# Routing by a sorted top-8 and a 32-wide weight row, with denominators moved inside SBUF and three stores moved, in a linear-attention and expert layer

## The reference, cut to what matters

```
x = x + layernorm(attention(layernorm(x)))
x = x + layernorm(ffn(layernorm(x)))

attention: q, k, v of 16 heads of 32; rope on q and k
  phi(t)  = exp(features(t) - |t|^2 / 2)          # 128 features for each head
  numer   = phi(q) @ sum_tokens(phi(k) v)
  denom   = max(phi(q) . sum_tokens(phi(k)), 1e-6)
  out     = (numer / denom) @ w_out.T

ffn: scores = sigmoid(X @ gate_w.T)               # 32 experts
  idx  = top_k(scores + bias, 4);  w = scores[idx] / sum(scores[idx])
  pos  = how many earlier (token, choice) pairs took the same expert
  kept = pos < 512                                # capacity of an expert
  out  = sum over kept choices of w * W2(silu(W1 x) * W3 x)  +  a shared expert
```

## Time and profile before

| | us |
|---|---|
| median of three runs (2088.13 to 2090.12) | 2089.63 |
| the profiled execution's own time | 2089.07 |
| its span, first to last instruction | 2087.3 |
| projection, about | 0 to 585 |
| sums over the keys, about | 585 to 830 |
| attention and routing, up to the last send | 830 to 1414 |
| experts, up to the landing of the last add | 1414 to 1892 |
| combination | 1892 to 2087 |

### The profile page before, as it was taken

The page is one execution under the profiler, slowest core; times in us unless marked ns, Lnnn a source line. Parts: engine busy times, 40 slices in busy tenths (PEclk is TensorE's granted clock), DMA queues, the critical chain, the costliest instruction groups (busy, mean ns, idle before and its releaser), DMA issues.

```text
span 2087.3 us, 33721 instructions
## 1 busy us (share of the span) xinstructions
PE 1819.7 (87%) x12976; PEld 889.0 (43%) x12976; DVE 1207.8 (58%) x2230; ACT 1124.8 (54%) x1371; POOL 758.3 (36%) x718
## 2 busy tenths in 40 slices
PE   8999999999969998897888887455999989987795
PEld 5444444444448785132333333222444444443331
DVE  6776767676620000376888898861444344445786
ACT  5565555555436665586778775513444444432443
POOL 0000000000000000015877787874777777761110
PEclk9999999999979999999999999777999999999997
DMA  7445444446368885768877775342999999987983
GB/s 249 165 137 184 143 177 143 178 139 212 107 173 211 211 212 133 171 206 180 244 220 222 230 221 186 137 171 79 203 206 234 242 241 241 202 147 243 344 292 129
DMA packets 188848, 405.15 MB, mean 194 GB/s; under 512 B 33812, under 2 KB 72084, under 8 KB 172064
## 3 DMA queue, kind: packets, MB, share of 16 engines
q1 hardware_dynamic: 83184, 222.41, 35.6%
q10 hardware_dynamic: 68640, 124.26, 17.3%
q0 software_dynamic: 36864, 56.32, 14.4%
HBM read 237.06 MB, written 177.08 MB: 198 GB/s over the span
## 4 chain that ended last, share of the span: by engine, by line
PE 13%; DMA 12%; DVE 12%; issue 10%; POOL 9%; ACT 4%; SPq 1%; POOLq 0%; DVEq 0%; ACTq 0%
POOL slot_dram L1260 4%; DMA acc_dram<-s_y,s_slot 3%; PE s_gates L1485 3%; PE s_ups L1485 3%; PE s_ys L1500 2%; DMA s_spread<-share_dram 2%; DMA s_rows<-rows_dram,s_slot 2%; POOL acc_dram L1426 2%; DMA den_dram<-s_den 2%; PE s_turned L1462 1%; DVE s_stats L1651 1%; ACT s_xT L1531 1%; DVE s_x L1670 1%; POOL s_rows L1412 1%; PE s_y L898 1%
## 5 line engine op out<-in xcount | busy, mean ns | idle before, releaser
L258 PE MATMUL s_proj<-s_xT,keep_wqkv 128*128 128x512 f16 x1536 | 341.8, 379 | 0.0
L1260 POOL DMA_INDIRECT slot_dram<-keep_filled,keep_slots x256 | 292.1, 1141 | 105.2 <-issue 74.4
L1426 POOL DMA_INDIRECT acc_dram<-s_y,s_slot x128 | 205.1, 1603 | 93.0 <-issue 35.6
L258 PEld LDWEIGHTS s_proj<-s_xT,keep_wqkv 128*128 128x128 f16 x1536 | 147.8, 98 | 183.2 <-issue 12.6
L898 PE MATMUL s_y<-keep_wo,s_at_hl 128*128 128x512 f16 x768 | 188.6, 398 | 36.9 <-ACT s_z L988 36.9
L1540 ACT ACTIVATE s_gate<-s_gates 128x512 f32<-128x512 f32 x96 | 57.1, 597 | 263.8 <-PE s_ups L1485 218.4
L1610 DVE SCALAR_TENSOR_TENSOR s_h<-s_gate,s_ups 128x512 f32<-128x512 f32 x96 | 65.9, 686 | 216.1 <-ACT s_gate L1540 216.1
L339 POOL TENSOR_SCALAR s_rstd<-s_mv 128x4 f32<-128x4 f32 x16 | 16.0, 998 | 458.9 <-DVE s_mv L354 458.9
L676 ACT ACTIVATE s_phi<-s_logits 128x1024 f32<-128x1024 f32 x128 | 131.1, 1024 | 83.9 <-PE s_logits L697 83.9
L237 PE MATMUL s_proj<-keep_wqkv,s_xT 128*128 128x512 f16 x768 | 173.8, 383 | 1.2 <-ACT s_xT L500 1.2
L967 ACT ACTIVATE s_phi<-s_logits 128x1024 f32<-128x1024 f32 x128 | 131.4, 1027 | 63.5 <-PE s_logits L867 62.6
(11 more groups left out here) (165 smaller groups left out, 3202.8 us busy)
## 6 DMA issues: line engine op xcount, KB each, us to landing
s_x<-x_in SPq DMA_DIRECT2D x32, 1024.0 KB, 11.9
qk_dram<-s_hl ACTq DMA_DIRECT2D x32, 1024.0 KB, 6.0
keep_ahead<-qk_dram SPq DMA_DIRECT2D x48, 512.0 KB
acc_dram<-s_zero SPq DMA_DIRECT2D x17, 1024.0 KB, 13.9
v_dram<-s_v ACTq DMA_DIRECT2D x16, 1056.0 KB, 6.9
s_v<-v_dram SPq DMA_DIRECT2D x16, 1056.0 KB, 11.2
s_spread<-share_dram SPq DMA_DIRECT2D x64, 256.0 KB
x_dram<-s_x ACTq DMA_DIRECT2D x16, 1024.0 KB, 5.6
```

Source lines behind the costliest of these rows:

```text
L258: mm = nc.tensor.matmul(out[:, 512 * b:512 * b + 512], left, right, start=(c == 0 and i == 0), stop=(c == EC - 1 and i == 2))
L1260: nc.gpsimd.indirect_dma_start(out=io["slot"], out_offset=bass.IndirectOffsetOnAxis(ap=slots[n % 2][:, a * K + j:a * K + j + 1], axis=0), ...
L1426: nc.gpsimd.indirect_dma_start(out=io["acc"], out_offset=bass.IndirectOffsetOnAxis(ap=slot[e % RING][:, a, 0:1], axis=0), in_=y[e % 2][:, ...
```

## The change

What is computed stays the same; the data that the last two stages hand over has another shape.

- **Top four by replacement.** `choose` takes the eight largest values of a row (as before), then replaces the four largest of them in a copy with a marker (`match_replace`, whose list of eight is the top four and four markers) and compares the copy with the marker: this gives the 0/1 mask of 32 experts without the indices, the 128 x 512 one-hot tile and its sum.
- **Weights as a row of 32.** `weigh` multiplies scores by the mask and divides by the sum. The 32 weights are stored behind the token's row in DRAM (`store_weights`), which grows from 2048 to 2176 bytes. In the expert stage a new DVE copy, `take_weight(e)`, takes column e of the gathered rows.
- **Destinations by sorting.** For each expert the value 2^20 - 512 e - position is formed, 0 where the token isn't kept; the eight largest, subtracted from 2^20, are the destinations. The slot holds the token alone, 4 bytes. `filled` is gone.
- **Denominators from SBUF to SBUF.** They are put on every eighth partition, and one DMA brings them from `den` to `dens`.
- **Steps.** FILL and SEND go from 21 to 20; the stores of x1 and rows are issued one step later (4n + 16, 4n + 18); the weights are stored in step 4n + 22. `STEPS` falls from 85 to 84.

```diff
-        SCORE, CHOOSE, PLACE, WEIGH, FILL, SEND = 18, 18, 19, 19, 21, 21
+        SCORE, CHOOSE, PLACE, WEIGH, FILL, SEND = 18, 18, 19, 19, 20, 20
...
-                for i in range(HPC):
-                    sp.dma_start(io["den"][n, i], den[D * i:D * i + EC, :]).then_inc(den_stored, 16)
-                sp.wait_ge(den_stored, 16 * HPC * (n + 1))
-                sp.dma_start(dens[:], io["den"][n].rearrange("i c (k q) -> (i c k) q", q=KP)).then_inc(dens_loaded, 16)
+                sp.dma_start(dens[:], den[0:P:D // EC, :]).then_inc(dens_loaded, 16)
...
+            def store_weights(n):
+                act.wait_ge(weights_ready, n + 1)
+                act.dma_start(io["rows"][n * G:(n + 1) * G, E:ROW].rearrange("(a p) n -> p a n", p=P),
+                              weights[n % 2][:].bitcast(U32)).then_inc(weights_stored[n % 2], 16)
...
-                n = group_at(s, A - 1 + ADD + 1)
+                n = group_at(s, A - 1 + ADD + 2)
                 if n is not None:
                     store_x1(n)
-                n = group_at(s, A - 1 + TURN + 1)
+                n = group_at(s, A - 1 + TURN + 2)
                 if n is not None:
                     store_rows(n)
...
+                n = group_at(s, WEIGH + 3)
+                if n is not None:
+                    store_weights(n)
...
                 for a in range(A):
-                    ins = nc.vector.max_index(index[:, a, :], top[:, a, :], biased[:, a, :])
+                    best = top[:, a, :].rearrange("p (b j) -> p b j", j=K)[:, 0:3:2, :]
+                    ins = nc.vector.match_replace(left_over[:, a, :], best, biased[:, a, :], NEVER)
                 then(ins)
-                then(nc.vector.tensor_copy(chosen[:], index[:, :, 0:K]))
-                then(nc.vector.tensor_tensor(onehot[:], number, chosen[:].unsqueeze(3).broadcast_to([P, A, K, NE]),
-                                             ALU.is_equal))
-                    ins = nc.vector.tensor_reduce(mask[:], onehot[:].rearrange("p a j e -> p a e j"), AX.X, ALU.add)
+                nc.vector.tensor_scalar(mask[:], left_over[:], NEVER, None, ALU.is_equal).then_inc(mask_ready, 1)
...
-                then(nc.vector.tensor_tensor(picked[:], onehot[:], per_choice(score[:]), ALU.mult))
-                then(nc.vector.tensor_reduce(w[:], picked[:], AX.X, ALU.add))
-                then(nc.vector.tensor_reduce(weight_sum[:], w[:], AX.X, ALU.add))
+                k = n % 2
+                dve.wait_ge(mask_ready, n + 2)
+                if n >= 2:
+                    dve.wait_ge(weights_stored[k], 16 * (n // 2))
+                then(nc.vector.tensor_tensor(weights[k][:], score[:], mask[:], ALU.mult))
+                then(nc.vector.tensor_reduce(weight_sum[:], weights[k][:], AX.X, ALU.add))
...
             def read_position(n):
+                at = position.rearrange("p (a e) -> p a e", e=NE)
                 dve.wait_ge(position_ready, n + 1)
-                nc.vector.tensor_copy(where[:].rearrange("p a e -> p (a e)"), position).then_inc(where_ready, 1)
+                nc.vector.tensor_tensor(away[:], first, at, ALU.subtract).then_inc(where_ready, 1)
+                nc.vector.scalar_tensor_tensor(out=taken[:], in0=at, scalar=float(CAP), in1=mask[:], op0=ALU.is_lt,
+                                               op1=ALU.mult).then_inc(where_ready, 1)
...
             def fill(n):
+                dve.wait_ge(where_ready, 2 * n + 2)
+                then(nc.vector.tensor_tensor(away[:], away[:], taken[:], ALU.mult))
+                nc.vector.tensor_reduce(ours[:], mask[:].rearrange("p a e -> p e a"), AX.X, ALU.add)
+                for a in range(A):
+                    ins = nc.vector.max(last[:, a, :], away[:, a, :])
+                then(ins)
                 if n >= 2:
                     dve.wait_ge(scattered[k], 16 * A * K * (n // 2))
+                nc.vector.tensor_scalar(slots[k][:].rearrange("p (a j) -> p a j", j=K), last[:, :, 0:K], -1.0, NOWHERE,
+                                        ALU.mult, ALU.add).then_inc(slots_ready, 1)
+                then(nc.vector.tensor_tensor(before_us[:], before_us[:], ours[:], ALU.add))
...
-                        in_=filled[n % 2][:].bitcast(U32)[:, a, j, :], in_offset=None, bounds_check=NSLOT - 1,
+                        in_=keep["token"][:, m:m + 1], in_offset=None, bounds_check=NSLOT - 1,
...
-        rows = [t.sb(f"rows{r}", [P, A, 2 * E], F16) for r in range(AHEAD)]
+        rows = [t.sb(f"rows{r}", [P, A, ROW], U32) for r in range(AHEAD)]
+        weight = [t.sb(f"weight{r}", [P, A]) for r in range(AHEAD)]
...
+            def take_weight(e):
+                r = e % AHEAD
+                dve.wait_ge(gathered[r], 16 * A * (e // AHEAD + 1))
+                if e >= AHEAD:
+                    dve.wait_ge(y_copied, A * (NS + e - AHEAD + 1))
+                nc.vector.tensor_copy(weight[r][:], rows[r][:].bitcast(F32)[:, :, E + e]).then_inc(weight_ready, 1)
...
                 for i in range(IC):
                     hidden(NS + e + 1, i)
                     low(NS + e + 1, i)
+                if e + 2 < NE:
+                    take_weight(e + 2)
                 down(e)
```

More of the change, by code:

```diff
@@ L780, in attend_and_route_programs @@
         power, eps = t.sb("power", [P, 2]), t.sb("eps", [P, 2])
-        slots, filled = keep["slots"], keep["filled"]
+        slots = keep["slots"]
         score, biased, grown = t.sb("score", [P, A, NE]), t.sb("biased", [P, A, NE]), t.sb("grown", [P, A, NE])
-        top, index, chosen = t.sb("top", [P, A, 8]), t.sb("index", [P, A, 8], U32), t.sb("chosen", [P, A, K])
-        onehot, picked = t.sb("onehot", [P, A, K, NE]), t.sb("picked", [P, A, K, NE])
+        top, left_over = t.sb("top", [P, A, 8 + K]), t.sb("left_over", [P, A, NE])
         mask = t.sb("mask", [P, A, NE], F16)
         before_us, ours = t.sb("before_us", [P, NE], F16), t.sb("ours", [P, NE])
-        where, slot, far, place = (t.sb("where", [P, A, NE]), t.sb("slot", [P, A, NE]), t.sb("far", [P, A, NE]),
-                                   t.sb("place", [P, A, K]))
-        w, weight_sum = t.sb("w", [P, A, K]), t.sb("weight_sum", [P, A])
+        away, taken, last = t.sb("away", [P, A, NE]), t.sb("taken", [P, A, NE]), t.sb("last", [P, A, 8])
+        weights, weight_sum = t.pair("weights", [P, A, NE]), t.sb("weight_sum", [P, A])
         logits = t.psum("logits", 2)
@@ L1070, in dve_program @@
         def dve_program(dve):
-            number = keep["expert"][:, 0:NE].unsqueeze(1).unsqueeze(1).broadcast_to([P, A, K, NE])
-            first = keep["expert"][:, NE:2 * NE].unsqueeze(1).broadcast_to([P, A, NE])
+            first = keep["expert"][:].unsqueeze(1).broadcast_to([P, A, NE])
             bias = keep["bias"][:].unsqueeze(1).broadcast_to([P, A, NE])
@@ L1171, in weigh @@
                 then(nc.vector.tensor_scalar(weight_sum[:], weight_sum[:], 1e-12, None, ALU.max))
                 then(nc.vector.reciprocal(weight_sum[:], weight_sum[:]))
-                then(nc.vector.tensor_tensor(w[:], w[:], weight_sum[:].unsqueeze(2).broadcast_to([P, A, K]), ALU.mult))
+                nc.vector.tensor_tensor(weights[k][:], weights[k][:], weight_sum[:].unsqueeze(2).broadcast_to([P, A, NE]),
+                                        ALU.mult).then_inc(weights_ready, 1)
             def read_position(n):
+                at = position.rearrange("p (a e) -> p a e", e=NE)
@@ L1182, in fill @@
[L1182 to L1187, removed]
@@ L1312, in expert_and_combine_programs @@
         x1 = [t.sb(f"x1{r}", [P, A, E]) for r in range(X1S)]
-        total = [y[0][:], y[1][:]] + [r[:].rearrange("p a n -> p (a n)").bitcast(F32).rearrange(
-            "p (a e) -> p a e", a=A) for r in rows]
+        total = [y[0][:], y[1][:]] + [r[:].bitcast(F32)[:, :, 0:E] for r in rows]
         stats, mv = t.sb("stats", [P, A, 6]), t.sb("mv", [P, A, 2])
@@ L1684, in dve_program @@
                 copy_early(p)
+            take_weight(0)
             for i in range(IC):
@@ L1687, in dve_program @@
                 low(NS, i)
+            take_weight(1)
             for e in range(NE):
@@ L1767 @@
     "v": ([NG, P, A * H * (D + 1)], F32),
-    "den": ([NG, HPC, EC, G], F32),
     "share": ([NG, HPC, EC, G], F32),
@@ L1771 @@
     "xT2": ([NG, P, 2 * EC * G], F16),
-    "rows": ([T, 2 * E], F16),
-    "slot": ([NSLOT, 2], U32),
+    "rows": ([T, ROW], U32),
+    "slot": ([NSLOT, 1], U32),
     "acc": ([T + CAP, E], F32),
@@ L1777 @@
     "ident16": ([P, P], F16), "ident32": ([P, P], F32), "heads": ([P, D], F32),
-    "tri": ([P, P], F16), "ones": ([P, P], F16), "gate": ([P, EC * NE], BF16), "expert": ([P, 2 * NE], F32),
+    "tri": ([P, P], F16), "ones": ([P, P], F16), "gate": ([P, EC * NE], BF16), "expert": ([P, NE], F32),
     "bias": ([P, NE], F32), "token": ([P, NG * A], U32),
@@ L1788, in build @@
         keep["ahead_loaded"] = Tools(nc, ctx, "keep").sem("ahead_loaded")
-        for name, shape, dt in (("slots", [P, A * K], U32), ("filled", [P, A, K, 2], F32)):
```

(2 more changed lines are left out.)

68 lines of the change are left out of this document (33 added, 35 removed).

## The result

The changed kernel takes 2134.95 us (median of 4 runs, 2128.02 to 2138.0), the kernel before 2089.88 us (4 runs, 2088.13 to 2095.85): a ratio of 1.0206 with a 95% interval of 1.0172 to 1.0239. Forecast were 2061 us and a range of 2042 to 2084. The change makes the kernel 2% slower, and the prediction was wrong in its sign. The profiled execution took 2137.09 us with a span of 2135.3.

A forecast was written before the change was run, and what follows sets the result against it. POOL was taken to bound the attention stage, PE most of the experts' periods. From 2089.07 us, -4.5 (denominators), -2.6 (DVE), -7.0 (earlier step), -18 (waits) and +4 (experts) gave 2061 us, range 2042 to 2084.

The forecast's parts named there:

- Work that stays: POOL's 256 sends of 128 descriptors stay; data falling from 8 to 4 bytes was priced at nothing.
- rival 1: Attention stage: spread shares become the wait, `divide` stops, POOL starves, the 18 us gain goes; 2079 us, chance 0.14.
- On the way: POOL's waits for slots after the first send, 22.4 us, fall to 4: gain 18 us (bounds 8 and 22).
- The sign that the prediction named for this rival: For the spread-share rival: the first send starts early and the last does not end early.
- The one hop for den: Front of the attention stage: one transfer replaces 6.5 us of store and load, taking 2.0 us; gain 4.5 us.
- Stores: Later x1 and earlier-grouped rows stores stay hidden, rows landing in 5.4 us against 14; weights' small pieces cost nothing.
- Rival 2: Experts' stage: longer rows double a gather's packets and cost POOL more; slower, 2105 us, chance 0.10.
- Rival 3: Experts' stage bound by transfers, costing +21 us instead of +4; 2078 us, chance 0.11.
- Rival 4: POOL is freed more, as fewer small DVE products hit its sends: -18 us, 2043 us, chance 0.08.

The follow-up runs named there:

- e2: Changed kernel with slot entries of 8 bytes again (token and a zero) instead of 4: 2091.84 us, 1.0055 to the kernel before.
- e16: Kernel before with dense slot entries of 4 bytes, the tokens' weights replaced by 1: 2098.99 us, 1.0083 to the kernel before.
- e5: Changed kernel with FILL and SEND back at 21: 2109.64 us, 1.0148 to the kernel before.
- e11: Changed kernel with slot writes of 8 bytes, 64 bytes apart, the list now 1 MB: 2053.91 us, 0.985 to the kernel before.
- e14: Changed kernel with slot entries 64 bytes apart and the stores of x1 and rows at their old steps: 2058.58 us, 0.9868 to the kernel before.
- e13: Kernel before with its 8-byte pairs written 64 bytes apart: 2072.47 us, 0.9948 to the kernel before.
- e17: Changed kernel with slot entries 128 bytes apart: 2058.82 us, 0.9882 to the kernel before.

## Why the prediction was wrong

**The step that failed** is in "Work that stays": "the data falls from 8 to 4 bytes, but a send of 8 bytes takes 0.973 and a gather of 2048 bytes 1.001, so size is worth nothing". For POOL that is right: a send still takes 0.973 us. But a send's length on POOL says nothing of what its 128 writes do where they land. By the runs this term is not 0: from 64 bytes to dense entries of 4 the changed kernel loses 3.6% (1.0206 less 0.985, times 2082 us: 74 us). Of these, 1.5% (31 us) are the step from 8 bytes to 4 that the change makes, and 2.1% (43 us) the density that the old 8 bytes had already. In the kernel before, that density costs 0.5%, 10 us, which I had read as given. So this step alone is not the whole error: with the 8 bytes kept, e2 is at 1.0055 where 0.9863 was forecast. The second step is the price of rival 1. "On the way" counts POOL's waits for slots alone, and these came out well (1.0 us); its waits for variances, which were expected not to grow, went from 64.0 us to 144.1.

**Why it hurt the changed kernel more.** The list alone costs the kernel before 1.35% between 64 and 4 bytes (1.0083 less 0.9948; 27 us by the medians 2098.99 and 2072.47), the changed kernel 3.6%. Rival 1 named the mechanism: `fill` has left the stretch between `share` and `divide`, and `choose` is shorter, so a late spread stops `divide`, then POOL. I gave it 0.14 and 2079 us because I let the spread be only 3 us late; it was up to 17.31 us under way, behind a share store of up to 16.33. Given its place and its chain, the price had to be open upwards, and the range with it. The sign that the prediction named for this rival is what came: the first send early, the last not. In e16, where the cover is still there, `divide` waits 17.7 us; in the changed kernel 98.0. e5 puts `fill` back in its place: 58.2, and 0.6% less time. These runs fit the missing cover as the reason for the difference. That it is the only reason was not shown, since the sends' place in time moves with `fill`.

**What was right,** each in the changed kernel itself: first send 940.2 (938.6); `choose` down from 4.72 to 3.1 (3.0); `weigh` 1.24 (1.3); `fill` 1.2 to the slots (1.3); slots waited for once, 1.0 us (4); 472.7 us from first gather to last add (472.6); `take_weight` 0.162 (0.2); a gather 1.001 us.

**Sizes that were off.** The one hop for den lands in 4.97 us, just above the upper of its bounds (1.75 and 4.76), not in 2.0. The reciprocal of the shares starts 2.9 us earlier than before, not 4.5. "Stores" had the rows land in 5.4 us with 14 us of room. Issued beside xT2 they land in 14.1 us (median of 960 to 1300 us), and ACT waits for them once, 5.2 us. The list is not the cause of that: they take 13.1 us in e11 too, and 9.4 in e14, where they go at their old step. By the times of e11 and e14 it cost nothing.

**With the list out of the way the total comes out, but partly by luck.** e11 differs from the changed kernel in the list alone. Forecast for the change: 2061/2089.63 = 0.9863; e11: 0.985 (0.9814 to 0.9887). Its sends run from 940.3 to 1379.7, forecast were 938.6 to 1382. But e11 is set against a kernel before that still has its dense list. Against e13, where both lists are spaced, the change is worth 18.6 us (2072.47 less 2053.91), not 28: the first send comes 11.7 us earlier (952.0 to 940.3), and on the way to the last only 3.5 us are won (442.9 to 439.4), not 18. For the waits for slots that "On the way" meant to remove fall to 8.9 us in e13 by the spacing alone. So the gain of the other edits was real but smaller than forecast, and it was overrun by what the list costs.

**The other rivals.** Rival 2 fell: a gather takes 1.001 us, and q0 has 36864 packets in both kernels, with 57.69 MB instead of 56.32. By this count two rows of 2176 bytes do still go in one packet; the rule of the Trainium skill (DMA: Bandwidth & Descriptors, SWDGE vs HWDGE vs iDMA), a preference for 4096 bytes at most, doesn't show here. Rival 3 fell with the 472.7 us. Rival 4 fell: a send takes 1134 ns on the mean (290.4 us for 256) against 1141, 1.8 us in all, so the small products that went had held POOL up little: in the kernel before 35 sends ran beside one of them, 30 in under 1 us, the longest in 1.26.

## What to carry to other kernels

In this kernel an indirect store had two costs: what it takes on the engine that issues it, and what its writes do to other transfers in flight. The second showed in no duration of the store itself, but in other queues' transfers: compare the landing times of a small, regular transfer before and during the scatter. Try giving scattered entries room, 64 bytes here, before packing them tighter to save bytes; the loads that read the list back were cheap (the first took 1.78 us in e11 and 1.56 in the kernel before, and e11 is the fastest of all). When an edit takes work away from between the issue of a transfer and its use, price that transfer at its worst landing, not at its usual one. And when a fix speeds up the changed kernel, give the kernel before the same fix: only then is it known what the change itself is worth.

## What was not expected of the hardware

Around 955 us, with the sends writing 4-byte entries to a dense list, 80 packets of 2 KB of another queue held 16 engines for 5 us. Such stretches go with the spacing of the list. Of the 87 stretches of 5 us from 940 to 1375 us, those with a DMA share of 0.9 or more and under 150 GB/s are 6 in the changed kernel (the lowest at 33 GB/s), 1 in e2 (53), and none in e11 and e17; in the kernel before there is 1 (144), in e16 there are 2 (the lowest at 74), and in e13 none. The store of 32 KB of shares issued at 943.74 needed 16.33 us, though nearly all of its packets ran in the first two. Transfers of the changed kernel, 944 to 946 us and 946 to 952.8:

```profile
q1 hardware_dynamic: 143, 0.03, 20.4%
```

```profile
q0 software_dynamic: 133, 0.00, 1.5%
q1 hardware_dynamic: 1, 0.00, 0.0%
```

In the second stretch of 6.8 us the engines do next to nothing (1.5% of their time), and yet the store isn't complete. That speaks for writes held up behind the engines, at the memory, and not for a lack of engine time, but no run shows where they are held. What collides there stays open: only the spacing (4, 8, 64 and 128 bytes) and, at a spacing of 8 bytes, the width of the write (4 and 8) were varied. The runs show that spacing counts, and that width doesn't at 8 bytes of spacing. The list grew with the spacing, from 64 KB at 4 bytes to 1 MB at 64, so whether it is the distance between entries or the size of the whole list that counts was not told apart.
